# Distances of two heads as two products of 64 rows in place of one product of 128 rows with zero-padded queries

## The chip, the cores and the metric
The kernel runs on 1 core of a Trainium2 chip. The time is the device time of one execution in microseconds (us), over the whole program. The engines are TensorE (PE; its weight loads are listed apart as PEld), VectorE (DVE), ScalarE (ACT), GpSimd (POOL) and SyncE (SP), which here only issues transfers.

## The reference
The input is `x` of 32 batches x 256 tokens x 128 features. One transformer layer is computed: attention with 16 heads of 8 dimensions, then a mixture of four experts, each with a residual.

```
x = x + attn(layernorm(x));  x = x + experts(layernorm(x))

q, k, v  = layernorm(x) @ w_qkv.T, in 16 heads
a        = q @ k.T * scale;  a = a - max(a, axis=-1)      # 256 x 256 for each head
s(a)     = 1 + a(1 + a/2 (1 + a/3))  for a >= 0,  1 / (1 - a(1 - a/2 (1 - a/3)))  for a < 0
attn     = (s(a) / sum s(a)) @ v @ w_out.T + b_out
experts  = sum over the 2 best of 4 experts: gate_e * ((silu(h @ w1_e) * (h @ w3_e)) @ w2_e)
```

After the maximum is taken off, `a` is never positive, so only the second form of `s` is needed. The kernel calls the difference max - a the distance.

## The kernel before, in words
A batch is worked on over four steps of one software pipeline. Step n has a first half and a second half, each written out by hand for every engine, and all engines run in order. In the first half, PE computes the distances of batch n, the up projections of the experts of batch n-2 and the output projection of batch n-1. In the second half, PE computes the scores of batch n+1 (for the maxima), the down projections of batch n-2 and the weighted values of batch n. Steps 2 to 31 have the settled order, and they make up nearly the whole time: 30 steps.

Distances need more exactness than one fp32r product gives. So queries and keys are each split into a high and a low part, written to DRAM (`qk_scratch`), and read back so that one product sums all terms. Each head takes 64 rows of the array: its 8 dimensions lie 8 rows apart, the four terms (high and low of the query by high and low of the key) are rows 0 to 3 of each group of 8, and two spare rows hold the maximum (high and low part) on the side of the queries and ones on the side of the keys. `k_stack` holds 128 rows, two heads one above the other. There are 8 units of 2 heads (u = 0 to 7).

`q_pad` has the queries of the two heads side by side in 512 columns, head 0 in rows 0 to 63 of the first 256 columns, head 1 in rows 64 to 127 of the last 256; all other cells are zero, but for the two rows of the maxima (124 and 125), which serve both heads. One product of 128 rows x 128 keys x 512 columns (L1380) therefore gives the distances of both heads for 128 keys. A unit has two such products (c = 0, 1), and fills two PSUM banks.

How the distances stand on the engines:
- PE, `distances`, called in the first half. Units 0 and 1 follow each other, after the values (L1405) and ahead of weighted values (L1312, products of 128 rows x 32 columns, four beside each other in the array). Units 2 to 7 stand alone, each among up projections (L1294, 128 x 128 weights, 256 columns in fp32r) or transposes (L1427, L1436). From unit 2 on, unit u waits until DVE has done the polynomial of unit u-2.
- ACT squares a unit (L657), DVE computes the polynomial from the square and the distance (L906), and later ACT takes the logarithm and the exponential.
- DVE takes the maxima of the scores in the second half (L991) into `mx`; PE transposes them (L1613), DVE splits them into high and low part (L1038, L1040) in `m_split`, and SP sends them to the stack (L437). The first distances of the next first half wait for that transfer.
- SP reads the stacks from `qk_scratch`, in 4 transfers for `k_stack` and 8 for `q_pad` (L418) for each batch.

The scores (L1552) are the other products with part of the rows: four heads in four row groups of 32 rows, each with 128 columns of weights and 256 moving columns, each into a bank of its own.

Of the kernel before, what the change touches and what calls it, by code (L numbers as in the profile page):

```python
# [5 lines left out]
def attention_then_experts_kernel(nc: bass.Bass, x: bass.AP, w_qkv: bass.AP, w_out: bass.AP, b_out: bass.AP,  # L6
# [37 lines left out]
    TILE = 32  # L44
    TERMS = 4
    HALF = 64
    MROW = 124
    STEP = HALF // HD
    GP = H // 2
    UP = NB // 2  # L50
# [8 lines left out]
    with ctx:  # L59
# [27 lines left out]
        q_tile = sb("q_tile", [128, G, S], F32R)  # L87
        k_tile = sb("k_tile", [128, G, S], F32R)
        k_stack = [sb(f"k_stack{i}", [128, GP, S], F32R) for i in range(2)]
        q_pad = [sb(f"q_pad{i}", [128, GP, 2, S], F32R) for i in range(2)]  # L90
        ones = sb("ones", [2, S])
        v_pad = [sb(f"v_pad{i}", [128, C, H, 48]) for i in range(2)]
        mx = sb("mx", [128, H, C])
        m_split = sb("m_split", [64, 128], F32R)
        w_sq = sb("w_sq", [128, 2, 4 * S])
        poly = sb("poly", [128, U, 4 * S])
# [148 lines left out]
        stored = [sem(f"stored{i}") for i in range(2)]  # L245

        TILED = 16 * 2 * TERMS
        STACKED = 16 * 12
        RANK = 2 + E.bit_length() - 1
        GATE = 4  # L250

# [53 lines left out]
        def blank_stacks(eng, par):  # L305
            if par == 0:
                eng.wait_ge(xn_ok, 1)
            eng.memset(k_stack[par][:].bitcast(F32), 0.0).then_inc(blank[par], 1)
            eng.memset(q_pad[par][:].bitcast(F32), 0.0).then_inc(blank[par], 1)

        def tile_rows(tile, r):
            return tile[r::TERMS, :, :].bitcast(F32)
# [13 lines left out]
        def stack_part(part):  # L326
            return scratch[part].rearrange("(g e) t -> e g t", g=GP)

        def pad_rows(pad, r, j):
            return pad[HALF * j + r:HALF * (j + 1):STEP, :, j, :].bitcast(F32)  # L330

        def pad_part(part, j):
            return scratch[part].rearrange("(g j d) t -> j d g t", g=GP, j=2)[j]

        block = ctx.enter_context(nc.Block())

# [2 lines left out]
        def _(sp):  # L339
# [23 lines left out]
            def first_half(i, off):  # L363
                n = no(i, off)
                par = (off + 1) % 2
                y_from = address(n * S * D)
                split, scratch_read, w_used = value(n + 2), value(pair_count(i, off, STACKED)), value(U * n)
                scored, tiles_read = value(U * (n + 1)), value(TILED * n)
                stored_qk, res_used = value(16 * (n + 2)), value(n)
                gates_at, gated_before = value(16 * (n - 1)), value(UP * (n - 2))  # L370
                if isinstance(i, int) and n == -2:
                    sp.dma_start(x_in[:], batch_at(x, 0)).then_inc(x_loaded, 16)
                    other_weights()
                if has(i, off + 1):
                    after(sp, qk_ok, split)
                    after(sp, stacked[1 - par], scratch_read)
                    after(sp, tiled, tiles_read)
                    if isinstance(i, int) and n == 0:
                        sp.wait_ge(first_tiled[2], TILED)
                    if isinstance(i, int) and n == -1:  # L380
                        for r, part in enumerate((1, 3, 1, 3)):
                            sp.dma_start(tile_group(k_tile, r, 0), group_part(part, 0)).then_inc(first_tiled[0], 16)
                    sp.dma_start(scratch.rearrange("a p t -> p a t"),
                                 qk_split[:].rearrange("p a t -> p (a t)").rearrange(
                                     "p (a t) -> p a t", t=S).bitcast(F32)).then_inc(qk_stored, 16)
                if has(i, off - 2):
                    sp.wait_ge(gates_out, gates_at)
                    after(sp, gated, gated_before)
                    sp.dma_start(gate_all[:].rearrange("p t c e -> p (t c e)"),
                                 row_to_all(gate_scratch, 128 * C * E)).then_inc(gates_in, 16)  # L390
                if has(i, off + 1):
                    if isinstance(i, int) and n == -1:
                        for r, part in enumerate((1, 3, 1, 3)):
                            sp.dma_start(tile_group(k_tile, r, 1), group_part(part, 1)).then_inc(first_tiled[1], 16)
                    sp.wait_ge(qk_stored, stored_qk)
                    after(sp, s_full, scored)
                    for r, part in enumerate((1, 3, 1, 3)):
                        if isinstance(i, int) and n == -1:
                            sp.dma_start(tile_rows(k_tile, r)[:, 2:G, :],
                                         tile_part(part)[:, 2:G, :]).then_inc(first_tiled[2], 16)  # L400
                            continue
                        sp.dma_start(tile_rows(k_tile, r), tile_part(part)).then_inc(tiled, 16)
                    for r, part in enumerate((0, 0, 2, 2)):
                        if isinstance(i, int) and n == -1:
                            continue
                        sp.dma_start(tile_rows(q_tile, r), tile_part(part)).then_inc(tiled, 16)
                    after(sp, w_full, w_used)
                    if isinstance(i, int) and 0 <= n + 1 < 2:
                        sp.wait_ge(blank[par], 2)
                        sp.dma_start(k_stack[par][MROW:MROW + 2, :, :].bitcast(F32),  # L410
                                     ones[:].unsqueeze(1).to_broadcast([2, GP, S])).then_inc(ones_in[par], 16)
                    for r, part in enumerate((1, 3, 1, 3)):
                        if isinstance(i, int) and n == -1:
                            continue
                        sp.dma_start(stack_rows(k_stack[par], r), stack_part(part)).then_inc(stacked[par], 16)
                    for r, part in enumerate((0, 0, 2, 2)):
                        for j in range(2):
                            sp.dma_start(pad_rows(q_pad[par], r, j), pad_part(part, j)).then_inc(stacked[par], 16)  # L418
                if isinstance(i, int) and n == 1:
                    sp.dma_start(w2_sb[:], w2.rearrange("e (c p) d -> p (e c) d", p=128)).then_inc(ld_experts, 16)  # L420
                if has(i, off):
                    after(sp, xres_ok, res_used)
                    sp.dma_start(x_res[:], batch_at(x, y_from)).then_inc(xr_loaded, 16)

            def second_half(i, off):
# [7 lines left out]
                    sp.dma_start(x_in[:], batch_at(x, x_from)).then_inc(x_loaded, 16)  # L433
                if has(i, off + 1):
                    par = (off + 1) % 2
                    sp.wait_ge(m_ok, m_split_at)
                    sp.dma_start(q_pad[par][MROW:MROW + 2, :, :, :].bitcast(F32),  # L437
                                 m_split[:].bitcast(F32)).then_inc(m_stacked[par], 16)
                if has(i, off - 2):
                    par = off % 2  # L440
                    sp.wait_ge(acc_ok, added)
# [419 lines left out]
        def _(dve):  # L861
# [96 lines left out]
            def second_half(i, off):  # L958
# [28 lines left out]

                def scores_max(u):
                    dve.wait_ge(s_full, U * (n + 1) + u + 1)
                    by_row = mx[:].rearrange("p (g j) c -> p j c g", j=2)  # L990
                    nc.vector.tensor_reduce(by_row[:, :, :, u], score_buf[u].rearrange("p (j c t) -> p j c t", j=2, c=C),  # L991
                                            AX.X, ALU.min, negate=True).then_inc(s_used, 1)

                def queries_and_keys_copied():
# [39 lines left out]
                def maxima_out():  # L1034
                    m = n + 1
                    dve.wait_ge(mT_full, m + 1)
                    after(dve, m_stacked[off % 2], pair_count(i, off, 16))
                    nc.vector.tensor_scalar(m_split[:], misc[0:64, 0:128], 1.0, None, ALU.add).then_inc(mx_hi_ok, 1)  # L1038
                    dve.wait_ge(mx_hi_ok, m + 1)
                    nc.vector.scalar_tensor_tensor(m_split[32:64, :], misc[32:64, 0:128], 1.0,  # L1040
# [236 lines left out]
        def _(pe):  # L1277
# [19 lines left out]
            def weighted_values(i, off, g):  # L1297
# [10 lines left out]
                first = 16 - 16 * (g % 2)  # L1308
                for c in range(C):
                    for j in range(4):  # L1310
                        at = (2 * c + j % 2) * S
                        last = nc.tensor.matmul(pv[32 * j:32 * j + 32, g // 2, :],  # L1312
                                                v_pad[par][:, c, 4 * g + j, first:first + 32],
                                                poly[:, 2 * g + j // 2, at:at + S], start=(g % 2 == 0 and c == 0),
# [49 lines left out]
            def distances(i, off, u):  # L1364

                m, par = no(i, off), off % 2
                if u == 0:
                    pe.wait_ge(s_used, U * (m + 1))
                    pe.wait_ge(stacked[par], pair_count(i, off, STACKED))
                    pe.wait_ge(m_stacked[par], pair_count(i, off, 16))  # L1370
                    if isinstance(i, int) and 0 <= m < 2:
                        pe.wait_ge(ones_in[par], 16)
                elif isinstance(i, int) and m < 2:
                    if u > 2:
                        pe.wait_ge(poly_ok, U * m + u - 2)
# [1 line left out]
                    pe.wait_ge(poly_ok, U * m + u - 1)  # L1377
                dst = distance_buf(m, u)
                for c in range(C):
                    last = nc.tensor.matmul(dst[:, 2 * c * S:2 * (c + 1) * S], k_stack[par][:, u, c * 128:(c + 1) * 128],  # L1380
                                            q_pad[par][:, u, :, :].rearrange("p j t -> p (j t)"), start=True, stop=True)
                last.then_inc(w_full, 1)

            def first_half(i, off):
# [143 lines left out]
            def second_half(i, off):  # L1528
# [77 lines left out]
                def maxima_T():  # L1606
# [4 lines left out]
                        pe.wait_ge(xnT_ok, n + 3)  # L1611
                    for part in range(2):
                        last = nc.tensor.matmul(misc[32 * part:32 * (part + 1), 0:128],  # L1613
                                                   mx[:].rearrange("p h c -> p (h c)"), ident[:], start=True, stop=True)
                    last.then_inc(mT_full, 1)

                def queries_and_keys():
# [207 lines left out]
```

## Time and profile before

| | us |
|---|---|
| runs | 1124.59, 1124.82, 1122.79 |
| median | 1124.59 |
| the profiled execution: its time | 1123.23 |
| its span, first to last instruction | 1121.5 |
| PE busy | 1099.9 (98%) |
| ACT busy | 995.3 (89%) |
| DVE busy | 962.8 (86%) |
| POOL busy | 744.1 (66%) |

The granted TensorE clock was 0.998 of its full speed over the span. Busy time of an engine is the union of its instructions; matmuls are pipelined and their records overlap, so that the distance between the starts of two matmuls, and not the length of one, tells what one costs. The chain of waits is followed back from the last instruction; its pieces follow each other without a gap, so a piece's length is what the group adds to the time.

### The profile page before, as it was taken

The numbers are of one execution on the slowest core, as the hardware profiler recorded it, in microseconds if no ns is written. First come the engines' busy times: TensorE is split into PE (matmuls) and PEld (weight loads), VectorE is DVE, ScalarE is ACT, GpSimd is POOL, SyncE is SP. The second block draws the span as 40 slices with busy tenths as digits, with TensorE's granted clock in tenths as the row PEclk, the third lists the DMA queues.
The fourth block names the chain that finished last, engine by engine and source line by source line (L and its number), as shares of the span: only waits on it lengthen the run. The fifth ranks groups of instructions, "written<-read, shape, count | busy, mean of one in ns | idle before, by whom it ended". The sixth has DMA issues, their size and how long they took to land.

```text
span 1121.5 us, 29146 instructions
## 1 busy us (share of the span) xinstructions
PE 1099.9 (98%) x9968; PEld 934.8 (83%) x9968; DVE 962.8 (86%) x1665; ACT 995.3 (89%) x1034; POOL 744.1 (66%) x936
## 2 busy tenths in 40 slices
PE   6989999999999999999999999999999999999998
PEld 5768888888888888888888888888888888888888
DVE  5789888899888899888899988889988889998844
ACT  1789999999999999999999999999999999999982
POOL 4547766777676687776677767668767667776530
PEclk9999999999999999999999999999999999999999
DMA  6343433333433223343223343322433322344000
GB/s 192 110 143 120 129 105 96 95 103 122 123 115 101 90 87 122 123 128 105 90 88 110 118 127 114 98 91 90 122 123 123 107 88 88 113 122 125 30 7 10
DMA packets 130383, 117.49 MB, mean 105 GB/s; under 512 B 15748, under 2 KB 124964, under 8 KB 130340
## 3 DMA queue, kind: packets, MB, share of 16 engines
q1 hardware_dynamic: 128004, 113.78, 32.9%
q10 hardware_dynamic: 2336, 3.15, 0.9%
q8 instruction: 26, 0.43, 0.2%
q14 instruction: 17, 0.14, 0.0%
HBM read 94.18 MB, written 21.09 MB: 103 GB/s over the span
## 4 chain that ended last, share of the span: by engine, by line
PE 93%; DVE 3%; ACT 1%; ACTq 1%; DMA 1%; issue 0%; POOL 0%; SPq 0%; POOLq 0%; DVEq 0%
PE banks L1294 33%; PE banks L1569 20%; PE sc L1380 11%; PE banks L1312 11%; PE sc L1552 4%; PE misc L1294 2%; PE banks L1603 2%; DVE mx L991 1%; PE misc L1427 1%; PE misc L1445 1%; PE misc L1405 1%; PE banks L1552 1%; PE sc L1294 1%; PE banks L1288 1%; DVE poly L906 1%; PE sc L1745 1%
## 5 line engine op out<-in xcount | busy, mean ns | idle before, releaser
L481 POOL TENSOR_TENSOR hid<-hid,gate_all 128x512 f32<-128x512 f32 x240 | 380.7, 1630 | 167.6 <-DMA gate_all<-gate_scratch 156.8
L906 DVE SCALAR_TENSOR_TENSOR poly<-w_sq,sc 128x1024 f32<-128x1024 f32 x252 | 303.5, 1215 | 46.3 <-ACT w_sq L657 46.1
L1294 PE MATMUL banks<-xn_hi,w_hi 128*128 128x256 f32 x976 | 289.5, 297 | 0.3
L1294 PE MATMUL banks<-xn_lo,w_hi 128*128 128x256 f32 x976 | 275.2, 282 | 0.0
L1294 PE MATMUL banks<-xn_hi,w_lo 128*128 128x256 f32 x976 | 274.1, 281 | 0.0
L657 ACT ACTIVATE w_sq<-sc 128x1024 f32<-128x1024 f32 x252 | 255.6, 1027 | 13.0 <-PE sc L1380 7.0
L1569 PE MATMUL banks<-w_sb,hid 128*128 128x128 f32 x1920 | 245.9, 281 | 0.4 <-POOL hid L481 0.4
L766 ACT ACTIVATE poly<-poly 128x2048 f32<-128x2048 f32 x128 | 240.2, 1899 | 0.3
L1569 PEld LDWEIGHTS banks<-w_sb,hid 128*128 128x128 f32 x1920 | 223.3, 191 | 16.5 <-POOL hid L481 0.6
L771 ACT ACTIVATE poly<-poly 128x2048 f32<-128x2048 f32 x128 | 236.8, 1896 | 0.0
L991 DVE TENSOR_REDUCE mx<-sc 128x4 f32<-128x1024 f32 x192 | 229.4, 1211 | 6.5 <-PE sc L1552 5.7
L1294 PEld LDWEIGHTS banks<-xn_hi,w_hi 128*128 128x128 f32 x976 | 183.3, 188 | 37.2 <-issue 24.3
L666 ACT ACTIVATE silu_a<-banks 128x512 f32<-128x512 f32 x240 | 144.1, 600 | 60.9 <-PE banks L1294 44.5
L1294 PEld LDWEIGHTS banks<-xn_lo,w_hi 128*128 128x128 f32 x976 | 183.8, 188 | 5.1
L1294 PEld LDWEIGHTS banks<-xn_hi,w_lo 128*128 128x128 f32 x976 | 184.2, 189 | 0.0
L898 DVE TENSOR_TENSOR hid<-silu_a,banks 128x512 f32<-128x512 f32 x240 | 161.0, 681 | 16.5 <-ACT silu_a L666 16.0
L1380 PE MATMUL sc<-q_pad,k_stack 128*128 128x512 f32 x504 | 161.2, 411 | 1.5 <-DMA q_pad<-m_split 0.8
L1312 PE MATMUL banks<-poly,v_pad 128*32 128x256 f32 x2048 | 130.6, 384 | 0.9 <-DVE mx L991 0.7
L1312 PEld LDWEIGHTS banks<-poly,v_pad 128*32 128x32 f32 x2048 | 56.7, 109 | 50.6 <-issue 17.9
L1380 PEld LDWEIGHTS sc<-q_pad,k_stack 128*128 128x128 f32 x504 | 78.8, 189 | 9.2 <-issue 1.9
L991 DVE TENSOR_REDUCE mx<-banks 128x4 f32<-128x1024 f32 x64 | 77.6, 1212 | 0.0
L1552 PE MATMUL sc<-k_tile,q_tile 32*128 32x256 f32 x768 | 64.6, 328 | 4.2 <-DVE mx L991 3.7
(186 smaller groups left out, 1338.2 us busy)
## 6 DMA issues: line engine op xcount, KB each, us to landing
qk_scratch<-qk_split SPq DMA_DIRECT2D x32, 512.0 KB, 3.1
q_pad<-qk_scratch SPq DMA_DIRECT2D x256, 64.0 KB
k_tile<-qk_scratch SPq DMA_DIRECT2D x124, 128.0 KB, 2.5
q_tile<-qk_scratch SPq DMA_DIRECT2D x124, 128.0 KB, 2.5
k_stack<-qk_scratch SPq DMA_DIRECT2D x124, 128.0 KB
gate_all<-gate_scratch SPq DMA_DIRECT2D x30, 512.0 KB, 4.4
x_in<-in_L_attn_x_dram SPq DMA_DIRECT2D x32, 128.0 KB, 2.1
x_res<-in_L_attn_x_dram SPq DMA_DIRECT2D x32, 128.0 KB, 2.2
```

The lines of the kernel that those rows point to most:

```text
L481: nc.gpsimd.tensor_tensor(h, h, by_token.unsqueeze(1).to_broadcast([128, 2, C, 128]), ALU.mult).then_inc(gated, 1)
L657: nc.scalar.activation(w_sq[:, u % 2, :], distance_buf(n, u), ACT.Square).then_inc(sq_ok, 1)
L666: nc.scalar.activation(silu_a[:, u % 2, :], up_a[:], ACT.Silu).then_inc(silu_ok, 1)
L766: nc.scalar.activation(poly[:, C * g:C * (g + 1), :], poly[:, C * g:C * (g + 1), :], ACT.Ln, bias=2.0).then_inc(ln_ok, 1)
L771: nc.scalar.activation(poly[:, C * g:C * (g + 1), :], poly[:, C * g:C * (g + 1), :], ACT.Exp, scale=-1.0).then_inc(p_ok, 1)
L898: nc.vector.tensor_tensor(hid[:, 2 * u:2 * u + 2, :].rearrange("p a t -> p (a t)"), silu_a[:, u % 2, :], b_bank[u], ALU.mult).then_inc(hid ...
L906: nc.vector.scalar_tensor_tensor(poly[:, u, :], w_sq[:, u % 2, :], 3.0, distance_buf(n, u), ALU.add, ALU.mult).then_inc(poly_ok, 1)
L991: nc.vector.tensor_reduce(by_row[:, :, :, u], score_buf[u].rearrange("p (j c t) -> p j c t", j=2, c=C), AX.X, ALU.min, negate=True).then_i ...
L1294: last = nc.tensor.matmul(dst, lhs[a], rhs[b], start=(k == 0), stop=(k == len(terms) - 1))
L1312: last = nc.tensor.matmul(pv[32 * j:32 * j + 32, g // 2, :], v_pad[par][:, c, 4 * g + j, first:first + 32], poly[:, 2 * g + j // 2, at:at ...
L1380: last = nc.tensor.matmul(dst[:, 2 * c * S:2 * (c + 1) * S], k_stack[par][:, u, c * 128:(c + 1) * 128], q_pad[par][:, u, :, :].rearrange(" ...
L1569: last = nc.tensor.matmul(up_b[:, c * D:(c + 1) * D], hid[:, FB * e + f, c * 128:(c + 1) * 128], w2_sb[:, FB * e + f, :], start=(e == 0 an ...
```

## The change
`q_pad` becomes `q_stack`, with the same form as `k_stack`: 128 rows, two heads one above the other, 256 columns, no padding. A unit has four products in place of two: for each half c of the keys and each head j, the 64 rows of that head (weights of 64 rows x 128 columns) against 256 columns. The results of head j now go to bank j, so that the two heads of a c write to different banks; the readers of `poly` take the new order. Each head has its own rows for the maxima (60 and 61, 124 and 125). They are sent in two transfers, the high part as soon as it is there, the low part after it, and `mx` is kept in the order that this needs. The queries are read in 4 transfers of 128 KB in place of 8 of 64 KB, the ones in two in place of one, and the blanking of the query stack covers half the columns.

```diff
-        q_pad = [sb(f"q_pad{i}", [128, GP, 2, S], F32R) for i in range(2)]
+        q_stack = [sb(f"q_stack{i}", [128, GP, S], F32R) for i in range(2)]
-        mx = sb("mx", [128, H, C])
+        mx = sb("mx", [128, 2, GP, C])
-        STACKED = 16 * 12
+        STACKED = 16 * 8
+        MAXIMA = 16 * 2
...
+        def maxima_row(stack, part):
+            return stack[MROW + part::HALF, :, :].bitcast(F32)
...
                     for r, part in enumerate((0, 0, 2, 2)):
-                        for j in range(2):
-                            sp.dma_start(pad_rows(q_pad[par], r, j), pad_part(part, j)).then_inc(stacked[par], 16)
+                        sp.dma_start(stack_rows(q_stack[par], r), stack_part(part)).then_inc(stacked[par], 16)
...
+                    sp.wait_ge(mx_hi_ok, m_split_at)
+                    sp.dma_start(maxima_row(q_stack[par], 0), m_split[0:32, :].bitcast(F32)).then_inc(m_stacked[par], 16)
                     sp.wait_ge(m_ok, m_split_at)
-                    sp.dma_start(q_pad[par][MROW:MROW + 2, :, :, :].bitcast(F32),
-                                 m_split[:].bitcast(F32)).then_inc(m_stacked[par], 16)
+                    sp.dma_start(maxima_row(q_stack[par], 1), m_split[32:64, :].bitcast(F32)).then_inc(m_stacked[par], 16)
...
-                        at = (2 * c + j % 2) * S
+                        at = (C * (j % 2) + c) * S
...
                 for c in range(C):
-                    last = nc.tensor.matmul(dst[:, 2 * c * S:2 * (c + 1) * S], k_stack[par][:, u, c * 128:(c + 1) * 128],
-                                            q_pad[par][:, u, :, :].rearrange("p j t -> p (j t)"), start=True, stop=True)
+                    for j in range(2):
+                        rows, at = slice(HALF * j, HALF * (j + 1)), (C * j + c) * S
+                        last = nc.tensor.matmul(dst[:, at:at + S], k_stack[par][rows, u, c * 128:(c + 1) * 128],
+                                                q_stack[par][rows, u, :], start=True, stop=True)
                 last.then_inc(w_full, 1)
```

## Rows read from the trace of the kernel before

**Rows 1.** The page's chain that ended last, its share of the span by engine.
```profile
PE 93%; DVE 3%; ACT 1%; ACTq 1%; DMA 1%; issue 0%; POOL 0%; SPq 0%; POOLq 0%; DVEq 0%
```

**Rows 2.** Busy time in one settled step: length, PE, PEld, DVE, ACT, POOL, clock.
```profile
568.04:601.24 33.20, 33.18 (x307) 28.19 (x306) 29.77 (x52) 30.93 (x33) 23.58 (x30) 1.00 0.33 108
```

**Rows 3.** The chain of waits, first half: start us, us, what.
```profile
618.33 0.93 PE sc L1380 x4
619.26 1.00 PE banks L1312 x16
620.26 1.63 PE banks L1294 x12
621.89 0.46 PE sc L1380 x2
...
623.06 0.46 PE sc L1380 x2
623.52 1.42 PE banks L1294 x12
624.95 0.59 PE sc L1380 x2
...
626.69 0.58 PE sc L1380 x2
```

**Rows 4.** The chain of waits, second half of the step before.
```profile
601.24 0.44 PE misc L1445 x4
601.68 0.44 PE sc L1552 x8
602.12 1.98 PE banks L1569 x16
604.10 0.32 PE banks L1552 x2
604.42 0.00 PE sc L1552 x2
604.42 0.11 PE banks L1552 x2
604.53 0.01 PE sc L1552 x2
604.54 2.88 PE banks L1569 x24
...
610.50 1.09 PE banks L1569 x8
```

**Rows 5.** Timeline of DVE and PE at distance units 4 and 5: start us, us, instruction.
```profile
623.53 1.22 DVE L906 SCALAR_TENSOR_TENSOR poly<-w_sq,sc 128x1024 f32<-128x1024 f32 x1 [0.58 <-ACT w_sq L657]
...
624.67 0.28 PE L1294 MATMUL banks<-xn_hi,w_lo 128*128 128x256 f32 x1
...
624.81 0.73 PE L1380 MATMUL sc<-q_pad,k_stack 128*128 128x512 f32 x2
```

**Rows 6.** Timeline of DVE, SP and PE's weight loads at the maxima of one step.
```profile
613.92 0.28 DVE L1038 TENSOR_SCALAR m_split<-misc 64x128 fp32r<-64x128 f32 x1 [0.19 <-PE misc L1613]
...
614.55 0.61 SPq L437 DMA_DIRECT2D q_pad<-m_split  x1
...
618.06 0.76 PEld L1380 LDWEIGHTS sc<-q_pad,k_stack 128*128 128x128 f32 x4
```

**Rows 7.** The chain of waits at the start: the transfer of the maxima, and what follows.
```profile
55.94 2.84 DMA q_pad<-m_split
...
59.02 1.17 PE sc L1380 x4
```

**Rows 8.** One line's instructions, the query transfers on SP's queue: ns min/median/max.
```profile
L418 SPq DMA_DIRECT2D q_pad<-qk_scratch x256: 567/567/1123, 21.3 to 1033.8; - x128
```

More of the change, by code:

```diff
@@ L46, in attention_then_experts_kernel @@
     HALF = 64
-    MROW = 124
+    MROW = 60
     STEP = HALF // HD
@@ L308, in blank_stacks @@
             eng.memset(k_stack[par][:].bitcast(F32), 0.0).then_inc(blank[par], 1)
-            eng.memset(q_pad[par][:].bitcast(F32), 0.0).then_inc(blank[par], 1)
+            eng.memset(q_stack[par][:].bitcast(F32), 0.0).then_inc(blank[par], 1)
         def tile_rows(tile, r):
@@ L327, in stack_part @@
             return scratch[part].rearrange("(g e) t -> e g t", g=GP)
[L329 to L333, printed above, removed]
+        def maxima_row(stack, part):
+            return stack[MROW + part::HALF, :, :].bitcast(F32)
         block = ctx.enter_context(nc.Block())
@@ L409, in first_half @@
                         sp.wait_ge(blank[par], 2)
-                        sp.dma_start(k_stack[par][MROW:MROW + 2, :, :].bitcast(F32),
-                                     ones[:].unsqueeze(1).to_broadcast([2, GP, S])).then_inc(ones_in[par], 16)
+                        for part in range(2):
+                            sp.dma_start(maxima_row(k_stack[par], part),
+                                         ones[:].unsqueeze(1).to_broadcast([2, GP, S])).then_inc(ones_in[par], 16)
                     for r, part in enumerate((1, 3, 1, 3)):
@@ L989, in scores_max @@
                     dve.wait_ge(s_full, U * (n + 1) + u + 1)
-                    by_row = mx[:].rearrange("p (g j) c -> p j c g", j=2)
-                    nc.vector.tensor_reduce(by_row[:, :, :, u], score_buf[u].rearrange("p (j c t) -> p j c t", j=2, c=C),
+                    nc.vector.tensor_reduce(mx[:, :, u, :], score_buf[u].rearrange("p (j c t) -> p j c t", j=2, c=C),
                                             AX.X, ALU.min, negate=True).then_inc(s_used, 1)
@@ L1036, in maxima_out @@
                     dve.wait_ge(mT_full, m + 1)
-                    after(dve, m_stacked[off % 2], pair_count(i, off, 16))
+                    after(dve, m_stacked[off % 2], pair_count(i, off, MAXIMA))
                     nc.vector.tensor_scalar(m_split[:], misc[0:64, 0:128], 1.0, None, ALU.add).then_inc(mx_hi_ok, 1)
@@ L1369, in distances @@
                     pe.wait_ge(stacked[par], pair_count(i, off, STACKED))
-                    pe.wait_ge(m_stacked[par], pair_count(i, off, 16))
+                    pe.wait_ge(m_stacked[par], pair_count(i, off, MAXIMA))
                     if isinstance(i, int) and 0 <= m < 2:
-                        pe.wait_ge(ones_in[par], 16)
+                        pe.wait_ge(ones_in[par], 32)
                 elif isinstance(i, int) and m < 2:
@@ L1613, in maxima_T @@
                         last = nc.tensor.matmul(misc[32 * part:32 * (part + 1), 0:128],
-                                                   mx[:].rearrange("p h c -> p (h c)"), ident[:], start=True, stop=True)
+                                                   mx[:].rearrange("p j g c -> p (j g c)"), ident[:], start=True, stop=True)
                     last.then_inc(mT_full, 1)
```

## The prediction
> **What bounds the kernel now.** The page's chain that ended last comes first: PE holds 93% of the span, and no other engine more than 3% [rows 1]. The second view is the busy time of one settled step, a stretch of 33.20 us: PE 33.18, ACT 30.93, DVE 29.77 [rows 2]. So PE has no gap, the step is as long as PE's stream, and ACT sets a floor 2.3 us below it. The third view is the chain of waits through one step. Its pieces follow each other on PE, so the price of a group can be read directly. The distances (L1380) take 0.93 us for units 0 and 1 together, and then six pieces: 0.46, 0.46, 0.59, 0.58, and twice 0.46 again for units 6 and 7, like the first two [rows 3]. The sum is 3.94 us of the 33.2. A product of 512 columns thus costs 0.23 us. This is the only piece of PE's work that the change touches.
>
> **The products.** Here the trace has a near relative. The scores (L1552) are products of 32 rows, 128 columns of weights and 256 moving columns, and each goes to a bank of its own. In the chain a group of eight in two rounds of four shows as 0.32, 0.00, 0.11 and 0.01 [rows 4]. Two things are to be seen. The second round of four costs 0.12 in all, no more than one product of 256 columns (L1294: 1.42 us for 12, also 0.12 [rows 3]): products in different row groups run beside each other, and the weights of the second round are loaded under the first. And the first round costs 0.32, which is 0.20 more. That is the price of going from products over the whole array to products of a part: the earlier product must leave the array, and the weight load after it lies open.
>
> The way back costs the same. Behind a group of scores, 8 products of L1569 take 1.09 us, 16 take 1.98 and 24 take 2.88 [rows 4]. Eight more cost 0.89, so 8 alone should cost 0.89, and 0.20 is left over as a fixed part. L1312, which also cuts the array, shows it again: L1294 x12 takes 1.63 behind it, and 1.42 behind a product of the full array [rows 3], a difference of 0.21.
>
> Now the distances in the new form. A unit has two rounds (c) of two products (j) in different row groups and banks. I take 0.12 for a round and 0.20 for a switch of the array's form:
> - Units 2 to 7 stand among products of the full array. Each pays a switch, two rounds and a switch back: 0.20 + 0.24 + 0.20 = 0.64 us. Six make 3.84.
> - Units 0 and 1 together: one switch in, four rounds, 0.20 + 0.48 = 0.68. The way out costs nothing new, since L1312 behind them has another form anyhow, and pays for its own switch today (its 1.00 stays).
>
> The sum is 4.52 in place of 3.94 us: +0.58 a step, and 30 steps make +17.4 us. Half the streaming time is saved (3.94 to 1.92 with the waits of today in it), but 13 switches of 0.20 are paid for it, 2.6 us.
>
> Bounds. No row shows the 64-row form. For the switch the lower bound is zero, if halves of the array can be entered without emptying it; the upper is 0.20 with a little on it, from L1552. I take 0.20, since the weights have the same 128 columns as in L1552. The sum is steep here: a step costs 1.92 + 13 s against 3.94, so the two forms are level at s = 0.155 us, and each 0.01 us of s is 3.9 us of the time. For a round the lower bound is 0.12, the upper 0.24 (one after the other); I take 0.12, because four such products fit in it.
>
> **A wait that goes with it.** Units 4 and 5 take 0.59 and 0.58, not 0.46. The timeline says why: DVE's polynomial of unit 2 runs from 623.53 to 624.75, PE issues unit 4 at 624.81, and the product before it began at 624.67 [rows 5]. PE waits some 0.12 us for DVE. In the new form PE comes later to this place (a switch behind unit 2 and the whole extra of unit 3 lie between, some 0.4 us), while the distances of unit 2 are ready no later, as its rounds are shorter. I count both waits as gone; that is inside the sum, where 0.64 replaces 0.59. If they stayed, +0.25 a step, +7.5 us in all: 1149.
>
> The Trainium skill speaks of the switch too. "TensorEngine Tiling (Array Packing)", Key Properties, says that changing the tiling mode, and not just the tile, drains TensorE. It gives no price; its table counts 64 x 128 as a mode like 32 x 128, so by it the switch would be paid here as behind L1552, and the sum would be the one above. The trace agrees for the two forms that it has (0.20 and 0.21).
>
> "TensorE: Matmul & The Clock Gate", Part 3, states that a weight load overlaps matmuls in flight only when its row group differs. By that rule the second round of each unit would wait for its weights: nine loads a step, each some 0.1 us, and about 27 us more (an estimate from the half of the 0.20 above). The trace disagrees: the second round of L1552 uses the row groups of the first and costs 0.12, with nothing left over for a load.
>
> **The other edits.**
> - Maxima in two transfers. SP issues the one transfer at 614.55 and is held for 0.61 us [rows 6]; at the start of the program such a transfer takes 2.84 us from issue to landing [rows 7]. So it lands near 617.4, and PE loads the weights of unit 0 at 618.06 [rows 6]: cover of 0.65. The first new transfer can go 0.3 earlier, when L1038 ends at 614.20, the second is held behind it until about 614.85, and lands near 617.7: still 0.35 of cover. Cost 0 in the settled steps; behind it on SP stand the store of the output and of the gates, which nothing waits for within 0.3 us. In the first two steps the transfer lies in the chain [rows 7]: +0.3 each. If the landing took 0.5 longer, each step would lose 0.15: +4.5 us.
> - Queries in 4 transfers in place of 8: SP's queue is held 4 x 0.567 = 2.3 us less [rows 8]; the bytes are the same. SP is not in the chain. One issue more for the ones, in two steps of the fill: 0.
> - Half of the blanking on POOL, in the fill, under PE's and SP's work: 0. The new order in `mx`, in `poly` and of the banks changes no shape of an instruction on DVE, ACT or in L1312: 0.
> - In the fill, batch 1 gains a little (four products of L1380 at 1.17 behind a wait [rows 7], where no full switch is paid, would take some 0.6 less), against the 0.6 of the two transfers. I take 0 within 1 us.
>
> The profiled execution took 1123.23 us, of which 1121.5 are the span; with 17.4 on it, 1140.6. The median of the runs is 1.4 above that execution. I forecast 1141.
>
> **The rivals.**
> - *Halves without a switch.* If a 64-row product can follow a 128-row one as freely as another 128-row one, a step takes 1.92 in place of 3.94 for the distances. PE's stream falls by 2.0 to 31.2 us, but ACT is busy for 30.93 [rows 2] and not perfectly fed. I put the step near 31.8, 1.4 less, 42 us in 30 steps: 1082. For it speaks that the halves are a coarser cut than 32 rows; against it that both cut forms in the trace pay. The side turns at a switch of 0.155 us. "TensorEngine Tiling (Array Packing)", Performance Considerations, counts up to 2x for contractions of 64 rows or less; by that alone the 42 us would come.
> - *A cheaper switch.* If only the open weight load is paid, about 0.10, a step takes 1.92 + 1.3 = 3.22, 22 us less: 1102. For it: the 0.20 is a sum of two things, and one of them could be absent for halves. Against it: L1552 loads as many columns and pays both.
> - *No two beside each other.* If the two products of a round run in turn, 16 rounds cost 0.12 more, 1.9 a step, 58 us: 1199. The rounds of four in L1552 speak against it.
> - *The second transfer of the maxima becomes the wait.* It lands up to 0.5 us late: between 1141 and 1156.
>
> **How the numbers follow.** The forecast with both its variants (waits kept, smaller effects) 0.68, a late transfer 0.06, products in turn 0.04, a switch between 0.15 and 0.16, where the two forms are level, 0.04, a cheaper switch 0.08, none 0.10. A difference under 0.2% (2.2 us) can't be told from none. That makes slower 0.78, same 0.04, faster 0.18. The range goes from 1115, part of the way to the cheaper switch, up to 1157, the waits kept and a late transfer together; the likeliest case alone spans 1133 to 1149.
>
> **What would show it.** Right: in a settled step's chain the pieces of L1380 x4 at 0.44 and the group behind each 0.20 longer than today (L1294 x12 at 1.6 behind unit 3), x8 at 0.68; a step of 33.8 us; the 0.12 before units 4 and 5 gone; ACT's busy time as today and its share lower. Wrong: weight loads of L1380 that begin within 0.12 us of the product before them (no switch), rounds 0.24 apart (no two beside each other), or idle time of PE ahead of unit 0 that the transfer ends.

## The result, and the profile after

| | before | after |
|---|---|---|
| median of the runs | 1123.87 | 1131.72 |
| lowest and highest of 4 | 1122.79 to 1124.82 | 1130.68 to 1132.34 |
| span of the profiled execution | 1121.5 | 1129.9 |

The ratio is 1.0070, with a 95% interval of 1.0058 to 1.0083: 7.9 us slower, between 6.5 and 9.3. The forecast had the side right and the size wrong: +17 us, 1141. The granted clock was 0.998 in both profiles.

The length of a settled step can be read from one group that PE reaches once a step, the output projection (L1445 in both kernels). The view is the group's instructions: count, ns min/median/max, first and last start in us. First the kernel before, then the changed one.

```profile
L1445 PE MATMUL misc<-proj_T,attn_T x124: 271/275/377, 69.2 to 1065.0; 128*128 128x128 f32 x124
```
```profile
L1445 PE MATMUL misc<-proj_T,attn_T x124: 271/275/377, 68.2 to 1073.4; 128*128 128x128 f32 x124
```

30 steps lie between the first and the last: (1065.0 - 69.2) / 30 = 33.19 us before, (1073.4 - 68.2) / 30 = 33.51 after, so +0.31 a step and +9.4 in all. (Both lengths are 0.01 too long, since the last start is that of the fourth product of its group; this cancels in the difference.) The fill, the time ahead of the first output projection, is 1.0 shorter. Together that is the 8.4 us between the spans. The forecast had +0.58 a step.

Where it went is seen in the chain of waits. Here is the changed kernel's first half of one step (start us, us, what), to be laid beside [rows 3].

```profile
622.24 0.67 PE sc L1380 x8
...
625.54 0.43 PE sc L1380 x4
625.97 0.91 PE banks L1292 x6
626.87 0.43 PE sc L1380 x3
627.31 1.63 PE banks L1292 x12
628.93 0.43 PE sc L1380 x3
629.37 0.59 PE misc L1427 x4
629.96 0.72 PE banks L1292 x6
630.67 0.43 PE sc L1380 x4
631.11 2.35 PE banks L1292 x18
633.45 0.43 PE sc L1380 x4
633.89 0.37 PE misc L1436 x2
634.25 0.86 PE banks L1292 x6
635.12 0.43 PE sc L1380 x4
635.55 3.07 PE banks L1292 x24
```

(Some matmul records are missing, so a x3 stands for four.) And these are pieces of the same view of the kernel before, those that [rows 3] left out:

```profile
622.35 0.72 PE banks L1294 x6
...
625.54 0.44 PE misc L1427 x4
...
627.26 2.14 PE banks L1294 x18
629.41 0.46 PE sc L1380 x2
629.87 0.22 PE misc L1436 x2
...
630.10 0.98 PE banks L1294 x6
631.08 0.46 PE sc L1380 x2
631.53 2.88 PE banks L1294 x24
```

Laid side by side, per step in us:

| piece | before | forecast | after |
|---|---|---|---|
| L1380, units 0 and 1 | 0.93 | 0.68 | 0.67 |
| L1380, units 2 to 7 | 3.01 | 6 x 0.44 | 6 x 0.43 = 2.58 |
| extra in the group behind unit 2 | | +0.20 | 0.91 - 0.72 = +0.19 |
| behind unit 3 | | +0.20 | 1.63 - 1.42 = +0.21 |
| behind unit 4 (transposes) | | +0.20 | 0.59 - 0.44 = +0.15 |
| behind unit 5 | | +0.20 | 2.35 - 2.14 = +0.21 |
| behind unit 6 | | +0.20 | 1.23 - 1.21 = +0.02 |
| behind unit 7 | | +0.20 | 3.07 - 2.88 = +0.19 |
| sum against before | | +0.58 | +0.28 |

All lines but two are as forecast within 0.01 for each piece. Behind unit 4 it is 0.05 less, and behind unit 6, 0.18 less. (The pieces are rounded to 0.01 each; that is enough for the 0.03 between their sum and the length of the step.) The timeline of the kernel before shows why for unit 6 (start us, us, instruction):

```profile
629.25 0.62 PE L1380 MATMUL sc<-q_pad,k_stack 128*128 128x512 f32 x2
629.45 0.60 ACT L666 ACTIVATE silu_a<-banks 128x512 f32<-128x512 f32 x1 [1.11 <-PE banks L1294]
629.71 0.38 PE L1436 MATMUL misc<-ident,attn 128*128 128x128 f32 x2
...
630.09 0.19 PEld L1294 LDWEIGHTS banks<-xn_hi,w_hi 128*128 128x128 f32 x1 [0.24 <-ACT silu_a L666]
630.10 0.39 PE L1294 MATMUL banks<-xn_hi,w_hi 128*128 128x256 f32 x1
```

The two transposes start at 629.71 and 629.82, and the next product should follow 0.11 later, but starts at 630.10. It is up projection 6 (w1), which uses the same bank as up projection 5 and has to wait for ACT's SiLU of that, which ends at 629.45 + 0.60 = 630.05. The changed kernel at the same place:

```profile
633.38 0.50 PE L1380 MATMUL sc<-q_stack,k_stack 64*128 64x256 f32 x4
633.49 0.60 ACT L665 ACTIVATE silu_a<-banks 128x512 f32<-128x512 f32 x1 [1.26 <-PE banks L1292]
...
634.14 0.39 PE L1292 MATMUL banks<-xn_hi,w_hi 128*128 128x256 f32 x1
```

SiLU ends at 634.09, and up projection 6 starts at 634.14. From the start of SiLU to the start of up projection 6 it is 0.65 us in both kernels. Whatever PE does in between, here the whole of unit 6 with its switches, is free as long as it fits. The chain of waits gives all of this time to PE, and so did the forecast, which read from [rows 2] that PE has no gap.

The matmul records do hide it, because they overlap. The records of the weight loads do not: the row of PEld above says that it sat idle for 0.24 us until ACT's SiLU. The view of all waits has the sum over the whole kernel (us in total, times, longest us). For the kernel before:

```profile
PEld banks L1294 <- ACT silu_a L666: 7.4, 30, 0.3
```

That is 0.25 us in each of the 30 settled steps. In the changed kernel the same group is down to one wait of 0.6 us in the whole program: the changed unit 6 has filled the waits of the settled steps.

### The profile page after: what moved, and what is told of

It is laid out like the page before. It is cut to its first block, busy times and chain, and to the rows that moved or that the text cites. A ratio compares the mean times of both kernels' runs of the same rounds, so it can differ in the third digit from the quotient of the medians.

```text
span 1129.9 us, 30076 instructions
## 1 busy us (share of the span) xinstructions
PE 1108.3 (98%) x10480; PEld 924.8 (82%) x10480; DVE 966.2 (86%) x1665; ACT 988.5 (87%) x1034; POOL 736.7 (65%) x936
## 4 chain that ended last, share of the span: by engine, by line
PE 91%; DVE 3%; ACT 3%; ACTq 1%; issue 1%; DMA 0%; POOL 0%; SPq 0%; DVEq 0%; POOLq 0%
PE banks L1292 34%; PE banks L1569 20%; PE banks L1310 10%; PE sc L1380 9%; PE sc L1552 3%; PE misc L1292 2%; PE misc L1427 2%; PE banks L1603 2%; DVE mx L989 1%; PE misc L1445 1%; DVE poly L905 1%; PE misc L1405 1%; PE banks L1552 1%; PE sc L1292 1%; ACT poly L765 1%; PE misc L1436 1%
## 5 line engine op out<-in xcount | busy, mean ns | idle before, releaser
L1292 PE MATMUL banks<-xn_hi,w_hi 128*128 128x256 f32 x976 | 301.4, 309 | 0.2 <-ACT silu_a L665 0.2
L1380 PE MATMUL sc<-q_stack,k_stack 64*128 64x256 f32 x1008 | 118.1, 323 | 1.0 <-DVE poly L905 0.8
L1380 PEld LDWEIGHTS sc<-q_stack,k_stack 64*128 64x128 f32 x1008 | 73.0, 185 | 31.8 <-DVE poly L905 3.0
```

What stands on the lines that cost most here:

```text
L1292: last = nc.tensor.matmul(dst, lhs[a], rhs[b], start=(k == 0), stop=(k == len(terms) - 1))
L1380: last = nc.tensor.matmul(dst[:, at:at + S], k_stack[par][rows, u, c * 128:(c + 1) * 128], q_stack[par][rows, u, :], start=True, stop=True)
```

## The experiments

The theory after the result: the step pays about 0.20 for every change of the array's form, but the price depends on the place, and unit 6 stands in a wait that was there before. Rivals: the switch of the 64-row form is cheaper everywhere; the transfers have a part; the products of a unit do not run beside each other. "Step" is below always worked out as above, from the first and last start of the output projection. Every ratio is to the kernel before, timed beside the variant (medians 1122.9 to 1123.5); differences from the changed kernel's 1131.72 (there the kernel before had 1123.87) are good to about 1 us only. The granted clock was 1.00 in the settled steps of all the profiles from which steps are compared. Three dots in a diff stand for lines left out.

**The transfers alone.** The kernel before with only the maxima in two transfers.

```diff
-                    sp.wait_ge(m_ok, m_split_at)
-                    sp.dma_start(q_pad[par][MROW:MROW + 2, :, :, :].bitcast(F32),
-                                 m_split[:].bitcast(F32)).then_inc(m_stacked[par], 16)
+                    sp.wait_ge(mx_hi_ok, m_split_at)
+                    sp.dma_start(q_pad[par][MROW:MROW + 1, :, :, :].bitcast(F32),
+                                 m_split[0:32, :].bitcast(F32)).then_inc(m_stacked[par], 16)
+                    sp.wait_ge(m_ok, m_split_at)
+                    sp.dma_start(q_pad[par][MROW + 1:MROW + 2, :, :, :].bitcast(F32),
+                                 m_split[32:64, :].bitcast(F32)).then_inc(m_stacked[par], 16)
...
```


> The kernel before with only the maxima sent in two transfers (high part, then low part; products as before). Theory (the products are all of the 7.9 us): 0 within 1 us, since the trace of before leaves 0.35 us of cover behind the second transfer. Rival (the transfers cost part of it, at the start or in each step): +1 us or more, with idle time of PE ahead of unit 0.

Measured: 1123.89 against 1123.12, ratio 1.0008 (0.9999 to 1.0017). The interval holds no change, and up to 1.9 us of cost. The step is 33.22, 0.03 longer, which in one profile is within what the single steps scatter. So the transfers cost 0 to 1.9 of the 7.9 us, and about 6 at least are left for the rest of the change. The other small edits (the queries in 4 transfers, the ones in two, the blanking) were not run alone; the chain above puts the longer step on the products and on the groups behind them.

**The same extra work at two places.** In the kernel before, the first product of one unit is done twice, 0.23 us of PE's stream.

```diff
-                for c in range(C):
+                for c in ((0, 0, 1) if u == 7 else (0, 1)):
```


> The kernel before with the first product of unit 7 done twice in every batch (0.23 us more of PE's stream at that place). Theory (cover by other waits depends on the place; unit 7 has none): +0.23 x 32 = +7.4 us, the step 33.40 us. Rival (all places have the same slack, the shortfall of the forecast lies in a cheaper switch): the same +7.4 here and at unit 6.

> The same with unit 6. Theory: in the kernel before PE loads the first weights behind the transposes L1436 0.28 us after the last of them where 0.11 is usual, since it waits for the SiLU of up projection 5; 0.17 of the 0.23 us is hidden there, so +0.06 x 30 = +1.8 us, at most +3. Rival (no cover): +7.4 us as at unit 7.

Measured: unit 7 twice 1129.91, ratio 1.0061 (1.0048 to 1.0075), +6.8 us; unit 6 twice 1123.81, ratio 1.0005 (0.9996 to 1.0014), +0.7. The output projection, first with unit 7 and then with unit 6 done twice:

```profile
L1445 PE MATMUL misc<-proj_T,attn_T x124: 271/275/377, 69.0 to 1071.9; 128*128 128x128 f32 x124
```
```profile
L1445 PE MATMUL misc<-proj_T,attn_T x124: 270/275/377, 71.1 to 1067.3; 128*128 128x128 f32 x124
```

Steps of 33.43 and 33.21, +0.24 and +0.01. One and the same product costs its full 0.23 at unit 7 and next to nothing at unit 6. The chain shows where it is hidden (kernel with unit 6 done twice):

```profile
631.60 0.70 PE sc L1380 x3
...
632.51 0.75 PE banks L1294 x6
```

L1380 is 0.24 longer, and the six products behind the transposes take 0.75 in place of 0.98: the wait in front of them is used up, and PEld's 30 waits for the SiLU are gone from the view of waits, while with unit 7 done twice they still stand there with 7.4 us. I had expected that only 0.17 could be hidden; it was 0.22.

**Head by head.** The changed kernel with the four products of a unit in another order.

```diff
-                for c in range(C):
-                    for j in range(2):
+                for j in range(2):
+                    for c in range(C):
```


> The changed kernel with the four products of a unit in the order head 0 (both halves of the keys), head 1, in place of half by half. Theory (products in different row groups run beside each other, those in one row group in turn, and PE starts them in order): three rounds in place of two, +0.12 in each of 8 units, less where units 4 to 6 hide it; +0.6 to +0.9 a step, 1149 to 1158 us. Rival (the order does not matter, each row group works off its own products): 1132.

Measured: 1132.66, ratio to before 1.0082 (1.0066 to 1.0097); the changed kernel had 1131.72 and 1.0070, so the two intervals overlap. Pieces of its chain:

```profile
589.43 0.67 PE sc L1380 x8
...
592.73 0.44 PE sc L1380 x4
```

The theory of three rounds (1149 to 1158) fell: a unit still has two rounds (0.44), and not the three that a start in order would need. In the trace's records two products of a unit start within 0.01 us, and the other two 0.22 us later. So two products of one row group, issued one behind the other, do not keep the other head's products from running beside them. (The description of the kernel says that all engines run in order; for PE's products within a unit the two rounds speak against it.)

**No switch.** Two products of all 128 rows and 256 columns for each unit. This kernel leaves out the parting of the two heads: each of its distances is a sum over both, so its output is not that of the reference. ACT and DVE read the one bank of a unit twice, so their work keeps its size.

```diff
-                    for j in range(2):
-                        rows, at = slice(HALF * j, HALF * (j + 1)), (C * j + c) * S
-                        last = nc.tensor.matmul(dst[:, at:at + S], k_stack[par][rows, u, c * 128:(c + 1) * 128],
-                                                q_stack[par][rows, u, :], start=True, stop=True)
+                    last = nc.tensor.matmul(dst[:, c * S:(c + 1) * S], k_stack[par][:, u, c * 128:(c + 1) * 128],
+                                            q_stack[par][:, u, :], start=True, stop=True)
...
```


> The changed kernel with each unit as two products of all 128 rows and 256 columns (one for each half of the keys) into one bank, which ACT and DVE read twice; the two heads are summed, so the distances are not those of the reference. It streams 0.24 us a unit, as the changed kernel does, and the array keeps its form. Theory (what was paid is 13 switches of 0.20 us a step, partly hidden): PE's stream falls to some 31.2 us, and the step is then held by ACT (30.9) and by waits between the engines: 31.5 to 32.4 us, 1075 to 1102 us. Rival (the switch is not the cost, the number of products or loads is): over 1115 us.

Measured: 1095.36, ratio 0.9748 (0.9733 to 0.9763), 27.6 us under before and 36 under the changed kernel. It streams as many columns one after the other as the changed kernel (two times 256 a unit) and keeps the array's one form. It also has two products and weight loads a unit in place of four, so alone it does not part the switches from the number of products. The changed kernel's chain does: four products standing alone take 0.43, eight in a row 0.67, so four more cost 0.24, which is two rounds and nothing on top; and the groups behind a unit, whose products did not change in number, are 0.2 longer. The fixed part is paid for each change of form. The chain of the kernel without switches no longer lies on PE alone in the step:

```profile
617.95 2.98 ACT poly L768 x2
...
627.49 1.80 ACT poly L768
629.30 2.03 ACT poly L773 x2
```

ACT holds these parts of the second half. That fits why some 2 us less on PE bring only 27.6 / 30 = 0.9 a step, and why the forecast's rival of free switches (1082) was too low.

**Fewer switches by pairs of units.** In the changed kernel units 6 and 7 are put next to each other:

```diff
-                    distance(6)
                     attention_T()
-                    up_a_unit(i, off - 2, 6)
+                    distance(6)
                     distance(7)
+                    up_a_unit(i, off - 2, 6)
```


> The changed kernel with units 6 and 7 next to each other, ahead of up projection 6, and the transposes L1436 ahead of both: two switches a step less. Theory (a switch costs 0.20): unit 7 alone costs 0.64 less, and the stretch between up projections 5 and 6 is then 0.2 to 0.4 longer, as unit 7 there waits for the polynomial of unit 5: -0.25 to -0.45 a step, 1118 to 1124 us. Rival (new waits eat it): 1130 or more.

Measured: 1126.45, ratio 1.0027 (1.0016 to 1.0039), 5.3 us under the changed kernel, and still slower than before. The chain:

```profile
630.78 0.22 PE misc L1436 x2
631.00 0.76 PE sc L1380 x8
631.75 4.01 PE banks L1292 x30
```

From the transposes on, these pieces sum to 4.99 us; in the changed kernel the pieces from unit 6 on, in its chain above, sum to 5.16 (0.43, 0.37, 0.86, 0.43, 3.07). Two exits of a lone unit have become one, but the place of unit 6, which was free, is lost. And new waits came: the pair takes 0.76 and not the 0.67 of units 0 and 1, and the 30 products behind it take 4.01, where 24 took 3.07 and six more should make it 3.79; among them PEld waits 0.18 us for the SiLU of up projection 6. The net is 0.17 a step, less than the 0.25 to 0.45 expected, and the median is 2.5 us above the expected bounds. The direction is the theory's, the size is not.

The same with units 2 and 3 (behind up projection 2, the diff below), and then with all three pairs (units 4 and 5 too, behind up projection 4, with the transposes L1427 ahead of that projection):

```diff
                     ups(1)
-                    distance(2)
                     up_a_unit(i, off - 2, 2)
+                    distance(2)
                     distance(3)
```


> The changed kernel with units 2 and 3 next to each other, behind up projection 2: two switches a step less. Theory: -0.40 a step if DVE keeps up, 1120 us; the later start of unit 2 (0.9 us) may give back up to half: 1120 to 1127. Rival (ACT and DVE get unit 2 too late, and unit 4 waits for it): 1131 or more.

> The changed kernel with units 2 and 3, 4 and 5, 6 and 7 in pairs: seven switches a step in place of 13. Theory by switches alone: -1.2 a step, 1096 us. Each pair has to wait for both polynomials of the pair before it (two squares or one square, two polynomials and a SiLU product lie between, some 4.4 us, against 3.7 to 4.4 us of other PE work): waits of up to 0.7 us a pair, so 1100 to 1125. Rival (the alternation of single units was what fed ACT and DVE): slower than 1132.

Measured: 1148.48, ratio 1.0226 (1.0212 to 1.0240), and 1181.87, ratio 1.0518 (1.0504 to 1.0533). Both are on the rival's side, far above what the theory expected, for a reason that I had only half seen. The timeline behind units 2 and 3 in a pair, which PE issues at 634.43:

```profile
634.98 1.03 ACT L656 ACTIVATE w_sq<-sc 128x1024 f32<-128x1024 f32 x1 [1.03 <-PE sc L1380]
...
635.90 0.59 ACT L665 ACTIVATE silu_a<-banks 128x512 f32<-128x512 f32 x1
...
636.54 0.38 PE L1292 MATMUL banks<-xn_hi,w_hi 128*128 128x256 f32 x1 [0.46 <-ACT silu_a L665]
```

ACT works in order, and the square of unit 2 stands ahead of the SiLU of up projection 2. That SiLU now waits for the later unit, and PE waits for the SiLU. I then moved the SiLU ahead of the square on ACT, and the polynomial of unit 3 ahead of the product of hidden 2 on DVE, with pairs of 2 and 3 and of 6 and 7, and with the transposes L1427 ahead of unit 4:

```diff
                     values_T_copied()
-                    square(2)
                     silu(2)
+                    square(2)
                     square(3)
...
```


> The changed kernel with units 2 and 3 in a pair behind up projection 2, units 6 and 7 in a pair ahead of up projection 6, ACT's SiLU of up projection 2 ahead of the square of unit 2 and DVE's polynomial of unit 3 ahead of the product of hidden 2. Four switches a step less than the changed kernel. Theory: -0.40 for units 2 and 3 against the kernel with units 6 and 7 alone in a pair (33.30 us a step), of which a wait of unit 4 for DVE takes back 0.1 to 0.3: 33.0 to 33.2, 1117 to 1124 us. Rival (the two score buffers leave ACT and DVE too little lead for pairs): 1130 or more.

Measured: 1152.72, ratio 1.0265 (1.0251 to 1.0279), the rival's side again. The order on ACT was not all. The chain of this kernel:

```profile
604.29 1.03 ACT w_sq L656
...
605.43 1.23 DVE poly L905
...
606.70 0.50 PE sc L1380 x3
...
610.89 1.14 DVE poly L905
...
612.08 0.50 PE sc L1380 x4
```

Unit 4 waits for the square and the polynomial of unit 2, and unit 7 for the polynomial of unit 5: with two buffers a unit waits for the polynomial two units back, and single units leave DVE that time. Whether another order of all engines would bear pairs was not tried.

**Halves only where others pay for the switch.** Units 0 and 1 in halves, units 2 to 7 with padded queries as before; the maxima go to both stacks in four transfers.

```diff
+                    if u > 1:
+                        last = nc.tensor.matmul(dst[:, 2 * c * S:2 * (c + 1) * S],
+                                                k_stack[par][:, u, c * 128:(c + 1) * 128],
+                                                q_pad[par][:, u - 2, :, :].rearrange("p j t -> p (j t)"), start=True, stop=True)
+                        continue
                     for j in range(2):
                         rows, at = slice(HALF * j, HALF * (j + 1)), (C * j + c) * S
...
```


> Halves for units 0 and 1 alone, which stand ahead of products of another form anyhow; units 2 to 7 with zero-padded queries as before. The maxima go in four transfers, two for units 0 and 1 and two for the rest, which unit 2 waits for. Theory (a form change is worth it where several units share it): the pair costs 0.26 less a step, 12 switches go: -0.26 x 30 = -7.8 us on the kernel before, 1115 to 1117 us. Rival (a gain ahead of the weighted values is taken back by a wait on ACT's exponentials or on the transfers): 1121 to 1125.

Measured: 1117.24, ratio 0.9948 (0.9935 to 0.9962): 5.7 us faster than before, some 14 faster than the change, and 0.2 above the 1115 to 1117 expected. Its chain and its output projection:

```profile
615.54 0.67 PE sc L1405 x8
...
618.83 0.46 PE sc L1399 x2
```
```profile
L1470 PE MATMUL misc<-proj_T,attn_T x124: 271/275/377, 70.3 to 1059.0; 128*128 128x128 f32 x124
```

The pair costs 0.67 in place of 0.93, and all else in the step is as before. The step is 32.96, 0.24 less; 1.1 us are lost in the fill, where the first output projection comes at 70.3 and not at 69.2.

**One lone unit in halves, at two places.** The same kernel with a third unit in halves, 6 or 7, with transfers of its own for it.

```diff
-                    if u > 1:
+                    if u not in (0, 1, 6):
...
```


> Halves for units 0, 1 and 6, all others with padded queries. Theory (the switches around unit 6 fall in the time that PE waits for the SiLU of up projection 5 anyhow): no more than 0.02 us a step beside halves for units 0 and 1 alone, 1117 to 1118 us. Rival (each lone unit pays its two switches, 0.16 to 0.18): 1122.

> The same with unit 7 in place of unit 6: same number of products, transfers and switches, only the place differs. Theory: +0.165 a step, +5 us, 1122. Rival (places are alike): the same time as with unit 6.

Measured: 1124.30 with unit 6, ratio 1.0005 (0.9996 to 1.0014), and 1128.48 with unit 7, ratio 1.0043 (1.0029 to 1.0057). The output projection, unit 6 and then unit 7:

```profile
L1479 PE MATMUL misc<-proj_T,attn_T x124: 271/275/377, 77.5 to 1065.8; 128*128 128x128 f32 x124
```
```profile
L1479 PE MATMUL misc<-proj_T,attn_T x124: 271/275/377, 77.2 to 1070.5; 128*128 128x128 f32 x124
```

The steps are 32.94 and 33.11: unit 6 in halves costs nothing on top of units 0 and 1 (32.96), unit 7 costs 0.15, and 0.17 more than unit 6. The view of waits agrees. With unit 7 in halves PEld's waits for the SiLU of up projection 5 are still there, and with unit 6 in halves one of 0.7 us is left:

```profile
PEld banks L1317 <- ACT silu_a L686: 8.0, 31, 0.6
```

The difference of the medians, 4.2 us, is that of 30 steps (5.0) within their noise. The times themselves are 6 to 7 us above what I had expected, above the rival's 1122 too, so that the theory rests here on the steps and on the difference of the two, and not on the time of either. The excess lies in the fill: the first output projection comes at 77.5 in place of 70.3. I had not counted the additional transfers there, which SP issues one by one (0.6 us each) ahead of the first maxima: with unit 6 these start at 62.93 and not at 57.84, 5.1 later. Another 1.7 is the clock. PE had waited for the transfer, the granted clock of the stretch from 60 to 70 us is 0.69 (1.00 with units 0 and 1 alone), so a part of it ran at the lower of the two levels (1.2 and not 2.4 GHz), and the first three groups behind the wait take 1.22, 1.87 and 1.03 us in place of 0.73, 1.00 and 0.66.

## Why the prediction was right in its side and wrong in its size

- *The bound, and the price of a 512-column product* were read right: the pieces of the chain explain the step, +0.28 by their sum (rounded to 0.01 each) and +0.31 by its length. What was read wrong beside it is "PE has no gap": its weight loads waited 0.25 us a step.
- *A switch costs 0.20, also for 64 rows.* Right, though no row had shown it: 0.19, 0.21, 0.21 and 0.19 behind units 2, 3, 5 and 7. Behind unit 4 it was 0.15, where transposes follow, and so it is behind unit 6 ahead of the wait (0.37 against 0.22). "TensorEngine Tiling (Array Packing)", Key Properties, of the Trainium skill had said that any change of the mode drains TensorE, without a price. The trace agrees that the third form pays too.
- *Two products beside each other, weights loaded under the round before.* Right: x8 in 0.67 is 0.20 and four rounds of 0.12. The rule of the Trainium skill, "TensorE: Matmul & The Clock Gate", Part 3, that a weight load overlaps only with matmuls of another row group, does not hold here either.
- *"Units 2 to 7 stand among products of the full array. Each pays a switch, two rounds and a switch back: 0.64."* This is the step that failed, for unit 6. It was to add 0.18 (0.64 in place of 0.46). It added nothing: by the pieces 0.43 and 0.02 behind it in place of 0.46, since PE's wait of 0.25 for the SiLU of up projection 5 was already there. That is 0.18 x 30 = 5.4 of the 8.0 us by which the forecast for the settled steps was too high (17.4 against 9.4); shown by the same product at two places (+0.24 and +0.01 a step) and by halves at two places (unit 7 +0.15, unit 6 -0.01). I had looked for such waits in front of the distances, where units 4 and 5 stood out with 0.59 and 0.58, and not behind them: six products of L1294 took 0.98 there and 0.72 elsewhere. Nor had I used the row of PEld in the view of waits, which names the wait and its 7.4 us in the kernel before.
- *The waits ahead of units 4 and 5 go.* Right: both pieces are 0.43 now.
- *The other 2.6 us* are small errors in a steep term: some 0.01 on each of seven pieces of L1380, and 0.05 behind unit 4, where transposes follow. (By the rounded pieces these come to 0.12 a step, 3.6 us; the 1.0 too much is the rounding.) The prediction said that each 0.01 of the switch is worth 3.9 us, and its likeliest range (1133 to 1149) was still too narrow by 1.3 us.
- *The fill* was put at 0 within 1 us, and was 1.0 shorter. The run with the transfers alone has its first output projection at 68.2 too; which edit it was is open. That the two transfers are free in the settled steps is borne out only as far as the run with the transfers alone can tell, 0 to 1.9 us in the whole.

## What to carry to other kernels

Products with part of the rows run beside each other as hoped, but each change of the array's form costs a fixed time, so count the changes as well as the columns. Here halves paid where two units stand together next to other products that are cut already (the first two, -5.7 us), and not where units stand alone among products of the full array (+7.9 us for all). Moving units together to save changes did not pay: one pair won some 5 of the 7.9 us back, and the others cost more in waits between the engines than they saved. Before a fixed cost is multiplied by the number of its places, look behind each place as well as in front of it for a group that takes longer than the same group elsewhere, and read the waits of the weight loads (PEld) and not only those of PE: PE was busy for 33.18 of 33.20 us by its matmul records, and still waited 0.25 us a step by its weight loads, and that wait took the cost. Extra copies of one instruction at two places measure such a slack directly.

## What was not expected of the hardware

- The order of the four products of a unit does not matter: head by head they take 0.44 us as well, two rounds, though two products of one row group follow each other in the program. The Trainium skill, "TensorE: Matmul & The Clock Gate", Part 3, has matmuls start strictly in the order of the program; with that, by my estimate from the rounds of 0.12 and the switch of 0.20, three rounds would have been needed, 0.56. The trace does not agree.
- The switch back into transposes costs 0.15 and not 0.20 (0.59 against 0.44 for four of them, 0.37 against 0.22 for two).
